# A decoder layer on one core: a mask moved from TensorE products to a VectorE minimum, and one head's split moved ahead

## The reference

```python
gates = sigmoid((x @ w_gate).reshape(b, n, HEADS, EXPERTS).transpose(0, 2, 1, 3))
gm = one_hot(argmax(gates, -1), EXPERTS) * gates
values = einsum('bhne,ehdk,bnd->bhnk', gm, value_experts, x)
sim = einsum('bhid,bhjd->bhij', q * SCALE, k)            # 8 heads, 64 wide, n = 1024
sim = where(triu(ones((n, n)), 1), finfo.min, sim)       # causal
out = einsum('bhij,bhjk->bhik', softmax(sim, -1), values)
out = einsum('bhne,ehkd,bhnk->bhnd', gm, output_experts, out).sum(axis=1)
```

## Time and profile before

| | |
|---|---|
| median of 3 runs (lowest, highest) | 983.73 us (982.77, 984.59) |
| the profiled execution: time, span | 985.18 us, 983.4 us |
| busy PE, PEld | 924.0 us (94%), 711.3 us (72%) |
| busy DVE, ACT, POOL | 659.9 us (67%), 344.9 us (35%), 402.3 us (41%) |
| mean granted TensorE clock | 0.983 |

### The profile page before, as it was taken

One profiled execution on the slowest core, in us unless ns is written; L12 is line 12 of the kernel. 1 busy time (PEld: TensorE's weight loads), 2 busy tenths in 40 slices (PEclk: granted clock), 3 DMA queues, 4 the chain that ended last, 5 costly groups with the idle time before them and its releaser, 6 DMA issues.

```text
span 983.4 us, 15298 instructions
## 1 busy us (share of the span) xinstructions
PE 924.0 (94%) x5740; PEld 711.3 (72%) x5740; DVE 659.9 (67%) x1038; ACT 344.9 (35%) x628; POOL 402.3 (41%) x363
## 2 busy tenths in 40 slices
PE   6989999999888998999999998999998999989998
PEld 3568778887655554699975785888876556549998
DVE  4857666547665658499969575765676666658987
ACT  4635555020445544311124355630104445541000
POOL 6312322222777969647620032300035676773100
PEclk9999999999999999999999899999999999999999
DMA  6103000534244541368540000023222001124763
GB/s 211 49 9 122 2 1 8 168 97 131 77 141 141 168 140 46 83 193 215 177 138 1 1 1 1 2 69 109 64 82 59 12 12 39 38 69 127 200 192 103
DMA packets 52462, 86.06 MB, mean 88 GB/s; under 512 B 11127, under 2 KB 32343, under 8 KB 52391
## 3 DMA queue, kind: packets, MB, share of 16 engines
q1 hardware_dynamic: 51111, 80.91, 27.2%
q10 hardware_dynamic: 1280, 4.20, 1.9%
HBM read 61.39 MB, written 19.33 MB: 82 GB/s over the span
## 4 chain that ended last, share of the span: by engine, by line
PE 79%; DVE 10%; issue 4%; ACT 2%; DMA 2%; POOL 2%; SPq 1%; ACTq 0%; POOLq 0%; DVEq 0%
PE ps L1224 18%; PE ps L1568 10%; PE ps L1491 7%; PE ps L1574 5%; PE ps L1403 5%; PE ps L1232 4%; PE ps L1448 4%; PE ps L1355 3%; PE ps L1465 3%; PE ps L1537 3%; PE ps L1417 3%; DVE region L1097 2%; PE ps L1370 2%; PE ps L1538 2%; PE ps L1387 2%
## 5 line engine op out<-in xcount | busy, mean ns | idle before, releaser
L1097 DVE TENSOR_REDUCE region<-ps 128x1 f32<-128x512 f32 (+1 forms) x192 | 98.4, 551 | 72.0 <-PE ps L1468 71.1
L1141 DVE COPY_PREDICATED region<-region,ps 128x512 f32<-128x512 uint32 x112 | 81.8, 736 | 71.0 <-PE ps L1224 70.7
L1568 PE MATMUL ps<-expert_hi,kst 128*128 128x256 f32 x512 | 125.3, 283 | 1.1 <-DVE kst L1170 0.9
L1568 PE MATMUL ps<-expert_lo,kst 128*128 128x256 f32 x512 | 123.5, 279 | 0.0
L1170 DVE TENSOR_TENSOR kst<-region 128x1024 fp32r<-128x1024 f32 x64 | 84.2, 1316 | 41.2 <-PE ps L1540 22.8
L637 POOL TENSOR_TENSOR xT<-xT,region 128x896 f32<-128x896 f32 (+2 forms) x48 | 84.2, 1754 | 48.1 <-PE ps L1491 29.5
L1224 PE MATMUL ps<-expert_hi,wide_hi 128*128 128x512 f32 x256 | 102.7, 401 | 0.0
L1224 PE MATMUL ps<-expert_hi,wide_lo 128*128 128x512 f32 x256 | 100.2, 391 | 0.0
L1224 PE MATMUL ps<-expert_lo,wide_hi 128*128 128x512 f32 x256 | 99.8, 390 | 0.0
L1568 PEld LDWEIGHTS ps<-expert_hi,kst 128*128 128x128 f32 x512 | 96.1, 188 | 4.1 <-issue 4.1
L1568 PEld LDWEIGHTS ps<-expert_lo,kst 128*128 128x128 f32 x512 | 96.4, 188 | 0.0
(11 more groups left out here) (161 smaller groups left out, 1949.4 us busy)
## 6 DMA issues: line engine op xcount, KB each, us to landing
region<-hot_rows SPq DMA_DIRECT2D x128, 128.0 KB, 3.3
halves_kept<-expert_hi SPq DMA_DIRECT2D x16, 512.0 KB, 5.2
halves_kept<-expert_lo SPq DMA_DIRECT2D x16, 512.0 KB, 6.0
expert_hi<-halves_kept SPq DMA_DIRECT2D x64, 128.0 KB, 3.0
expert_lo<-halves_kept SPq DMA_DIRECT2D x64, 128.0 KB, 3.0
expert<-in_value_experts SPq DMA_DIRECT2D x8, 512.0 KB, 4.3
kx<-kst ACTq DMA_DIRECT2D x16, 256.0 KB, 3.0
expert<-in_output_experts SPq DMA_DIRECT2D x8, 512.0 KB, 4.4
```

Source lines behind the costliest of these rows:

```text
L1097: dve.tensor_reduce(mx[:, i, at_mx:at_mx + 1], ps[:, max_bank(h, m), 0:w], AX.X, ALU.max).then_inc(sem["s_max"], 1)
L1141: dve.copy_predicated(V3_heads[:, t], chosen.unsqueeze(3).broadcast_to([P, PAIRS3, 2, HD3]), ps[:, n % 4, :].rearrange("p (a i k) -> p a i ...
L1568: mm(ps[:, 4 + t // 2, t % 2 * D:(t % 2 + 1) * D], kst[n % 2][:, t * P:(t + 1) * P], w[:, slot, columns], start=(n == 0 and t % 2 == 0 and ...
```

## The change

- The product with `neg` on the transposed scores (line 1540) is gone. VectorE's new `mask_weights(h, j)` takes, in SBUF, the minimum of the diagonal 128x128 tile of the exponentials and a table that holds 0 where a weight must be 0 and 1e30 elsewhere (`neg[:, 1]` plus 1e30). `weigh` and `add_weights` wait for it (`pt_masked`).
- VectorE does the minima of head h among the maxima of head h + 1: tiles 0 and 1 before the maximum of score 0, tile 2 before that of score 5, tile 3 before 8, tile 4 before 11; tiles 5, 6, 7 after `max_row`. Those of head 7 come after everything else of the heads, ahead of the output stage's masked operands.
- `split(1)`, `queries_high(1)`, `keys_twice(1)` and `queries_low(1)` move from loop 0 into the values' stage (after n = 42, and beside it).
- Scores 7, 9 and 11 are computed a block earlier, the last projection at block 9 instead of 11, ScalarE's copies of the projections a block after each (`QK_OUT_AT`); the transposition waits for all four copies.
- `factors` moves from after `max_row` to after the maximum of score 6 (the last but one: among head 7's minima). SP stores the denominators of heads 0 and 1 one piece earlier.

```diff
-        SCORES_AT = {4: (0, 1, 2), 5: (3, 4), 6: (5, 6), 7: (7, 8), 8: (9, 10), 9: (11,)}
+        SCORES_AT = {4: (0, 1, 2), 5: (3, 4), 6: (5, 6, 7), 7: (8, 9), 8: (10, 11)}
         MAX_ROW_AT = 10
-        PROJECT_AT = (3, 5, 7, 11)
+        MASKED_BEFORE, MASKED_LATE = {0: (0, 1), 5: (2,), 8: (3,), 11: (4,)}, (5, 6, 7)
+        PROJECT_AT = (3, 5, 7, 9)
+        QK_OUT_AT = (4, 6, 8, 10)
...
+        SPLITS_FIRST = (PROJECT_FIRST + TT, PROJECT_FIRST + TT + 2)
...
-                if q == E3 + SPLIT_AT[3, 8]:
+                if q == E3 + SPLIT_AT[3, 3]:
                     keep_den(0, 0)
...
+                    if q == E3 - 1:
+                        queries_low(b, 1)
...
                     until(pool, "pt_ready", b, h * NB + LAST_BLOCK[j] + 1)
+                    until(pool, "pt_masked", b, h * TT + j + 1)
...
-                        queries_high(0)
+                        for h in range(2):
+                            queries_high(h)
                         keys_twice(0)
+                    if q == PROJECT_FIRST // TT + 2:
+                        keys_twice(1)
...
-                        if h + 1 < H3 and n == 0:
+                        if 0 < h < H3 - 1 and n == 0:
                             queries_high(h + 1)
...
-                        if n in PROJECT_AT and h % 2 == 0 and h + 2 < H3:
-                            qk_evac(h // 2 + 1, PROJECT_AT.index(n))
+                        if n in QK_OUT_AT and h % 2 == 0 and h + 2 < H3:
+                            qk_evac(h // 2 + 1, QK_OUT_AT.index(n))
...
+                def mask_weights(h, j):
+
+                    until(dve, "pt_ready", b, h * NB + FIRST_BLOCK[j] + 1)
+                    own = kept(b, h, j)[:, 0:P]
+                    dve.tensor_tensor(own, own, neg[:, 1, :], ALU.min).then_inc(sem["pt_masked"], 1)
...
-                    if n == PROJECT_FIRST + TT:
-                        split(0)
+                    if n in SPLITS_FIRST:
+                        split(SPLITS_FIRST.index(n))
...
                 for h in range(1, H3):
-                    split(h)
+                    if h >= 2:
+                        split(h)
                     for m in range(NB):
+                        for j in MASKED_BEFORE.get(m, ()):
+                            mask_weights(h - 1, j)
                         maximum(h, m)
                         if m == WEIGHTED_AFTER and h >= 5 and h % 2:
                             weighted(h - 5)
                             weighted(h - 4)
+                        if m == WEIGHTED_AFTER and h >= 4 and h % 2 == 0:
+                            factors(h // 2 - 2)
                     max_row(h)
-                    if h >= 4 and h % 2 == 0:
-                        factors(h // 2 - 2)
-                factors(PAIRS3 - 2)
+                    for j in MASKED_LATE:
+                        mask_weights(h - 1, j)
+                for j in range(TT):
+                    mask_weights(H3 - 1, j)
+                    if j == 1:
+                        factors(PAIRS3 - 2)
...
-                    until(pe, "qk_sb", b, min((h + 1) // 2 + 1, PAIRS3) * 2 * NC - (h % 2 and h + 1 < H3))
+                    until(pe, "qk_sb", b, min((h + 1) // 2 + 1, PAIRS3) * 2 * NC)
                     pe.transpose(ps[0:TT, 6, 0:P], mx[:, h % 2, 0:TT], ident).then_inc(sem["mxT_ps"], 1)
...
                     until(pe, "pt_ready", b, h * NB + LAST_BLOCK[j] + 1)
+                    until(pe, "pt_masked", b, h * TT + j + 1)
...
-                        last = mm(ps[:, bank, 0:w], kx[i][:, key], qx[i][:, query], start=False, stop=q0 > key_tile * P)
-                        if q0 == key_tile * P:
-                            last = mm(ps[:, bank, 0:P], ident_b[:, :], neg[:, 1, :], start=False, stop=True)
+                        last = mm(ps[:, bank, 0:w], kx[i][:, key], qx[i][:, query], start=False, stop=True)
```

More of the change, by code:

```diff
@@ L54, in decoder_layer @@
     NB = len(BLOCKS)
+    FIRST_BLOCK = [min(n for n, (x, _) in enumerate(BLOCKS) if x == j) for j in range(TT)]
     LAST_BLOCK = [max(n for n, (x, _) in enumerate(BLOCKS) if x == j) for j in range(TT)]
@@ L216, in decoder_layer @@
             s_ps=H3 * NB, s_max=H3 * NB, tile_max=H3, mxT_ps=H3, m_row=H3,
-            st_ps=H3 * NB, pt_ready=H3 * NB, av_used=H3 * TT, oT_ready=PAIRS3 * NC,
+            st_ps=H3 * NB, pt_ready=H3 * NB, pt_masked=H3 * TT, av_used=H3 * TT, oT_ready=PAIRS3 * NC,
             mo_hi_ready=NEP, mo_lo_ready=NEP,
@@ L228, in decoder_layer @@
                 "c2k_ps", "c2v_ps", "c2k_sb", "c2v_sb", "dve_step"))
-        rows_kept, gates_in, gate_cols_in, den_in, factors_kept, kx_in = (
+        rows_kept, gates_in, gate_cols_in, den_in, factors_kept = (
             ctx.enter_context(nc.semaphore(n)) for n in (
-                "rows_kept", "gates_in", "gate_cols_in", "den_in", "factors_kept", "kx_in"))
+                "rows_kept", "gates_in", "gate_cols_in", "den_in", "factors_kept"))
         x_in = [ctx.enter_context(nc.semaphore(f"x_in{i}")) for i in range(TT // 2)]
         mask_in = [ctx.enter_context(nc.semaphore(f"mask_in{i}")) for i in range(MASKS)]
+        kx_in = [ctx.enter_context(nc.semaphore(f"kx_in{i}")) for i in range(2)]
         den_kept = [ctx.enter_context(nc.semaphore(f"den_kept{i}")) for i in range(2)]
@@ L640, in _ @@
                 for h in range(H3):
-                    if h + 1 < H3:
+                    if 0 < h < H3 - 1:
                         queries_low(b, h + 1)
@@ L829, in keys_twice @@
                     act.dma_start(kx[i][own:own + HALF, :].bitcast(fp32), kst[i][own:own + HALF, :].bitcast(fp32)
-                                  ).then_inc(kx_in, 16)
+                                  ).then_inc(kx_in[i], 16)
                 def rounded(k):
@@ L875, in _ @@
                                        ).then_inc(sem["pt_ready"], 1)
-                        if h + 1 < H3 and n == 0:
+                        if 0 < h < H3 - 1 and n == 0:
                             queries_high(h + 1)
-                        if h + 1 < H3 and n == 1:
+                        if 0 < h < H3 - 1 and n == 1:
                             keys_twice(h + 1)
@@ L934, in _ @@
             dve.tensor_copy(ident_b[:, :], ident).then_inc(casts, 1)
-            dve.tensor_copy(neg[:, :, :], neg_f).then_inc(casts, 1)
+            dve.tensor_copy(neg[:, 0, :], neg_f[:, 0, :]).then_inc(casts, 1)
+            step(dve.tensor_scalar(neg[:, 1, :], neg_f[:, 1, :], 1e30, None, ALU.add))
             step(dve.memset(v2[:, :, :, HD2:V2W], 1.0))
@@ L1442, in project @@
                     until(pe, "qk_sb", b, p * 2 * NC + n)
-                    if n in (0, 2 * NC - 1) and p:
-                        until(pe, "m_row", b, 2 * p - 1 + (n > 0))
+                    if n == 0 and p:
+                        until(pe, "m_row", b, 2 * p - 1)
                     parts = [(w, x, i) for i in range(DA)
@@ L1528, in _ @@
                         until(pe, "s_max", b, H3 * NB)
-                    pe.wait_ge(kx_in, 16 * (b * H3 + h + 1))
+                    pe.wait_ge(kx_in[i], 16 * (b * PAIRS3 + h // 2 + 1))
                     until(pe, "qx_ready", b, h + 1)
```

## The result

The changed kernel takes 999.82 us (median of 4 runs, 998.8 to 1003.5) against 983.25 for the kernel before: ratio 1.0177, 95% interval 1.0145 to 1.021. It is 16.6 us slower; 1009 were forecast. The profiled execution took 999.62 us, span 997.8, granted clock 0.981.

What follows compares the result with a forecast made beforehand. TensorE held three quarters and more of the chain of waits, with VectorE setting each head's tail. The terms summed to +24.9 us on the profiled 985.18, 1010.1; less 1.45 for the timed median, forecast 1009 us, 8-in-10 range 970 to 1023.

Steps and rivals of the forecast that it cites:

- The branch with no split overtaken: Low case of the forecast: GpSimd takes no turn ahead of the next head's split on VectorE; 997 us.
- signs of being right: Tile 3's minimum 1.5 to 2 us; score 5 to transposition 6.7; split subtractions over 3; transposition waits for ScalarE, loops 2, 4.
- Mask products, -6.2: TensorE's 128 removed products pay only where TensorE sets the pace, by counted places: -6.2 us, ends 0 and -16.6.
- Split of head 1 early, -4.4: Loop 0: TensorE's waits for an exponential and for head 1's split both go, 2 x 2.2 = -4.4 us.
- Its price in the values' stage, +1.0: Values' stage: a second split so soon puts VectorE behind the four PSUM banks; +0.5 us per image, +1.0.
- Tile 3 in the tail, +13.2: Loops 1, 3, 5: tile 3's minimum waits for GpSimd's add, VectorE's tail grows by 2.2 us; 6 x 2.2 = +13.2.
- The projections, +5.4: Loops 0, 2, 4: projections end before the transposition, which waits for ScalarE's last copy; +5.4 us, ends -3 and +8.
- Splits overtaken, +16.3: After the transposition: masks wake GpSimd's adds ahead of VectorE's split, score 0 comes late; +16.3 us, ends 0 and 28.
- Loop 6, +2.0: Loop 6: two multiplications already in the tail, tile 3's minimum meets a waiting GpSimd; +1.0 us each, +2.0.
- the output stage, +1.0: Output stage: the first two masked operands queue behind head 7's minima; +1.0 us for both images.
- Loop 1 of the first image, -2.1: Loop 1 of the first image has a wait of 2.13 us like the overtaken splits' already, so -2.1 us.
- Denominators, -1.3: Storing the denominators of heads 0 and 1 one piece earlier removes a 1.31 us wait in the first image: -1.3.

Runs made afterwards that it cites:

- 981.95: The changed kernel without any minimum or the waits for them, so with neither minima nor mask products: 981.95 us, ratio 0.999.
- 982.78: The kernel before without the 128 mask products on the transposed scores, nothing else changed: 982.77 us, ratio 1.0004.
- the filled waits: The kernel before without mask products, with products nobody reads where TensorE waits for VectorE in the tail: 976.37 us, ratio 0.9925.
- 980.3: The changed kernel's order with the mask as products on TensorE as before and no minimum: 980.34 us, ratio 0.9985.
- 977.2: The kernel before with head 1's split, scores 7, 9, 11, `factors` and first denominators moved as in the change; mask products and projections as before: 977.18 us, ratio 0.9948.
- tile 3 early: The changed kernel with tile 3's minimum before the maximum of score 5 instead of score 8: 992.29 us, ratio 1.0122.
- 1008.3: The changed kernel with the last projection back at block 11, ScalarE's copies at each projection's block, transposition waiting for three copies: 1008.33 us, ratio 1.0263.
- 988.6: The changed kernel with tile 3's minimum before score 5, last projection back at block 11, minima of tiles 0 and 1 before score 3: 988.58 us, ratio 1.006.

## Why the prediction was right, and where it was not

The direction, the main mechanism and the range held; the forecast was 9 us too high. Two errors stood against each other, and that they cancelled in part is luck. The minima were put at 13.2 + 2.0 + 16.3 + 1.0 = 32.5 us and cost 17.9; the rest was put at 24.9 - 32.5 = -7.6 and came to -0.8 (981.95 against 982.78). The branch with no split overtaken gave 997, close to the 999.8, and owes that to the same luck: its mask products were worth nothing. Of the signs of being right three came true (tile 3's minimum at 1.5 to 2 us, in four of six loops; a longer tail, 6.2 us; the wait for ScalarE in loops 2 and 4) and one did not: no subtraction of a split lasts over 3 us, and score 0 waits for none.

- **Mask products, -6.2: wrong as a term.** The count of places was near (0.34 to 0.48 us a loop), but the end got nothing (-1.5 to +2.2 us by the interval). The step that failed is that a product out of a place where TensorE paces comes off the end: TensorE's waits in VectorE's tail became longer, and the slow clock after them cost as much. The link to the clock rests on two pairs of kernels (0.986 with products and 0.978 without, 0.992 and 0.985) and on the filled waits, of whose gain a part arises where no filler stands.
- **Split of head 1 early, -4.4: right** where the projections stay, 26.4 to 23.8 us in loop 0 in both images. In the changed kernel the projections' new order takes it back (25.6 and 26.6). **Its price in the values' stage, +1.0, was too small:** 0.9 us in the first image and 2.1 in the second. GpSimd was counted as idle there; in the second image its second low half holds up VectorE's cast.
- **Tile 3 in the tail, +13.2: right in place and mechanism** (1.65 of waiting forecast, 1.85 - 0.28 = 1.57 measured), too large in the sum, as four of six were blocked: undoing it shortened loops 1, 3 and 5 of both images by 8.9 us together and the median by 7.5.
- **The projections, +5.4:** the wait for ScalarE is there (1.05 us); with products kept the order costs 980.3 - 977.2 = 3.2. Beside minima it saves 8.5. The prediction saw it hide VectorE's tail; it also keeps GpSimd's low half off tile 0's minimum in the odd loops.
- **Splits overtaken, +16.3: the term that failed.** The step that each mask wakes an add that takes the turn ahead of VectorE's next operation did not happen in the loops shown: the three minima start some 0.2 us after one another, all three before the add, and the split went on among the adds, so that score 0 came at 6.1 us, not at 6.9 or 9.1. GpSimd's long operation fell behind the split, upon tile 0's minimum. Where GpSimd is still at earlier work at that moment, a minimum does lie 1.4 to 1.6 us (loops 2 and 4 of the first image, loop 6 with tile 3 early); TensorE waits for the split only with tile 3 early, up to 1.1 us (loop 6).
- **Loop 6, +2.0, and the output stage, +1.0: too small.** Loop 6 is 2.6 and 1.9 us longer in the two images than with products in the same order. No split is late in it; its first 5.1 and 3.3 us run at the lower clock. With tile 3 early the second image has no such stretch there, but the split is late (2.75 us). The way from loop 6's end to the output's third item grew by 1.7 and 1.6 us (25.0 to 26.6 in the second image).
- **Loop 1 of the first image, -2.1:** it is 4.7 us shorter (20.97 and 16.29). **Denominators, -1.3:** the wait is gone; its worth was not measured by itself.
- **Not priced:** `factors` blocked in the tails, and the clock.

## What to carry to other kernels

Price an operation on two SBUF tensors by what GpSimd does at that moment, not by its size: the same minimum cost 0.28 us ahead of the adds and 1.9 to 2.4 behind one of GpSimd's operations, and moving three minima a few places (1008.3 to 988.6 us) was worth more than the change itself. Ask of work taken off the bounding engine where its time goes: into a wait behind another engine it brings nothing, and on TensorE it can bring a slower clock after it. A move that looks like a mere cost (the projections) may be what keeps two engines apart, so undo the parts in pairs as well as singly.

## What the runs showed of the hardware that was not expected

- TensorE, busy for 2.05 of 3.90 us behind VectorE, then ran 3 us at the lower of its two clocks. With seven products that nobody reads in a wait of 2.2 us, the stretch after it ran at the upper one (0.50 and 1.00 above, one profile each).
- Short VectorE operations queued behind one another were not parted by a GpSimd operation that waited for the first of them: three minima started between 760.53 and about 760.93, the add at 760.97. Where GpSimd was still at earlier adds (loop 6 with tile 3 early) they were parted: the third lasted 1.37 us. (The Trainium skill, page "SBUF — State Buffer", section "SBUF: two separate sides", gives the shared port to whoever starts first, for the whole instruction; the 1.85, 2.36 and 1.77 us agree, and in loop 1 the first to start was VectorE.)
- The clock also fell, or did not, in parts that no kernel here changed (55 to 60 us, 550 to 560). In the kernel before it was 0.66 and 0.68 over these stretches, in the one without products and with its waits filled 1.00 in both; no edit here explains that.
